# Mixture-of-experts loop: VectorE computes the next pair's weight addresses ahead of its label and meta copies

## What is computed

```python
logits = tokens @ router_weight.T                  # 32 experts, 4 picked for each token
topk_idx, topk_w = _route(tokens, router_weight, router_bias)
gate_vals = silu(einsum('th,eih->tei', tokens, gate_w))
up_vals = einsum('th,eih->tei', tokens, up_w)
expert_out = einsum('tei,ehi->teh', gate_vals * up_vals, down_w)
mixed = (take(expert_out, topk_idx) * topk_w).sum(1)
out = layernorm(x + mixed + shared(x))
```

## Time and profile before

| what | value |
|---|---|
| time, median of 3 runs | 595.2 us (590.54 to 598.46) |
| span of the profiled execution (its own time; no other is listed for it) | 591.0 us |
| TensorE busy, matmuls | 557.3 us, 94% |
| VectorE busy | 372.0 us, 63% |
| ScalarE busy | 278.8 us, 47% |
| GpSimd busy | 289.8 us, 49% |
| mean granted TensorE clock | 0.988 |

### The profile page before, as it was taken

One profiled execution on the slowest core, in us unless ns is written; L12 is line 12 of the kernel. 1 busy time (PEld: TensorE's weight loads), 2 busy tenths in 40 slices (PEclk: granted clock), 3 DMA queues, 4 the chain that ended last, 5 costly groups with the idle time before them and its releaser, 6 DMA issues.

```text
span 591.0 us, 16304 instructions
## 1 busy us (share of the span) xinstructions
PE 557.3 (94%) x4916; PEld 437.1 (74%) x4917; DVE 372.0 (63%) x1250; ACT 278.8 (47%) x561; POOL 289.8 (49%) x301
## 2 busy tenths in 40 slices
PE   5989999999989999999969999999999999999985
PEld 2446578677665766675529999999999999887863
DVE  2032657698885887679544666666666665634774
ACT  2334453765837575253213555555555554530234
POOL 5000000654777765667741666666666665660221
PEclk9999999999999999999987999999999999999998
DMA  7999978987899799799423555555555554528996
GB/s 260 249 237 230 236 220 201 277 271 193 267 248 287 224 322 391 268 395 343 171 93 96 168 165 164 162 172 163 160 167 168 180 171 153 172 91 353 414 413 246
DMA packets 125820, 135.34 MB, mean 229 GB/s; under 512 B 76872, under 2 KB 107087, under 8 KB 125136
## 3 DMA queue, kind: packets, MB, share of 16 engines
q1 hardware_dynamic: 108288, 95.92, 54.3%
q0 software_dynamic: 12672, 34.10, 15.2%
q10 hardware_dynamic: 4816, 4.74, 2.3%
HBM read 74.79 MB, written 60.96 MB: 230 GB/s over the span
## 4 chain that ended last, share of the span: by engine, by line
PE 63%; DMA 15%; SPq 6%; issue 5%; POOL 4%; DVE 3%; ACT 2%; ACTq 0%; POOLq 0%; DVEq 0%
PE bank L933 54%; PE bank L1292 5%; DMA wgu_sb<-pick_rows 4%; DMA o_slots<-wgu_sb 4%; DMA wd_sb<-o_slots 3%; POOL expert_rows L534 3%; PE bank L1350 2%; DMA expert_rows<-stage,pos 2%; SPq L319 1%; SPq L328 1%; SPq L299 1%; PE bank L1348 1%; PE bank L981 1%; DMA q_slots<-wd_sb 1%; SPq L285 1%
## 5 line engine op out<-in xcount | busy, mean ns | idle before, releaser
L568 POOL DMA_INDIRECT pick_rows<-prod,ids x134 | 131.2, 979 | 93.9 <-ACT prod L885 46.2
L534 POOL DMA_INDIRECT expert_rows<-stage,pos x128 | 129.1, 1008 | 57.0 <-issue 34.8
L933 PE MATMUL bank<-prod 128*128 128x128 f32 x1088 | 135.0, 278 | 1.0 <-issue 1.0
L933 PEld LDWEIGHTS bank<-prod 128*128 128x128 f32 x1088 | 128.9, 195 | 1.7 <-issue 1.6
L933 PE MATMUL bank<-wd_sb,wqkv_sb 128*128 128x512 f32 x192 | 91.5, 614 | 6.5 <-DMA wqkv_sb<-in_wqkv 5.9
L1754 DVE COPY prod<-wgu_sb 128x512 f32 x136 | 54.1, 440 | 54.5 <-issue 51.8
L885 ACT ACTIVATE prod<-bank,kept 128x256 f32<-128x256 f32 x136 | 57.0, 470 | 37.7 <-PE bank L933 35.1
L933 PEld LDWEIGHTS bank<-wgu_sb 128*32 128x32 f32 x2048 | 58.6, 136 | 16.8 <-issue 13.6
L933 PE MATMUL bank<-wd_sb,prod 128*128 x272 | 70.1, 380 | 0.8 <-DVE prod L1785 0.8
L933 PE MATMUL bank<-wgu_sb 128*32 128x64 f32 x2048 | 65.8, 296 | 2.2 <-DMA wgu_sb<-k_slots 2.2
L933 PEld LDWEIGHTS bank<-wd_sb,wqkv_sb 128*128 128x128 f32 x192 | 35.1, 194 | 41.6 <-issue 35.8
(11 more groups left out here) (148 smaller groups left out, 774.6 us busy)
## 6 DMA issues: line engine op xcount, KB each, us to landing
prod<-expert_rows SPq DMA_DIRECT2D x136, 132.0 KB
wgu_sb<-pick_rows SPq DMA_DIRECT2D x32, 512.0 KB, 14.7
wgu_sb<-in_wgu SPq DMA_DIRECT2D x2, 2560.0 KB, 13.4
expert_rows<-pad_rows SPq DMA_DIRECT2D x4, 1056.0 KB, 19.0
wd_sb<-in_xT SPq DMA_DIRECT2D x8, 512.0 KB, 4.8
q_slots<-wd_sb SPq DMA_DIRECT2D x16, 256.0 KB
k_slots<-wd_sb SPq DMA_DIRECT2D x16, 256.0 KB
wgu_sb<-q_slots SPq DMA_DIRECT2D x16, 256.0 KB
```

The lines of the kernel that those rows point to most:

```text
L534: pool.indirect_dma_start(xs, bass.IndirectOffsetOnAxis(ap=pos[e % 2][:, i, k:k + 1], axis=0), stage[:, i, k, :], None, bounds_check=XROWS ...
L568: pool.indirect_dma_start(z, bass.IndirectOffsetOnAxis(ap=index[:, j:j + 1], axis=0), rows[:, j, :], None, bounds_check=TOPK * NTOK - 1, o ...
L933: return pe.matmul(dst, lhsT, rhs, start=(k == 0), stop=(k == n - 1))
```

## The change

The register part of `copy_weights` becomes a function of its own, `find_weights`, which loads the packed word and holds the offsets of both tiles in registers. In a pair's body it is called first. The label is no longer the last step of the body, for pair n-1, but follows `find_weights` in the next body, for pair n-2; then come the keep, the meta copy and the weight copies. The last labels stand behind the loop.

```diff
+            def find_weights(quad, slot):
                 word = quad_experts(dve, quad)
+                return [dve.snap(dve.to_reg(expert(word, slot + j) * (KC * 2 * EI)), min_val=0,
+                                 max_val=(NE - 1) * KC * 2 * EI) for j in range(2)]
+
+            def copy_weights(n, par, found):
                 if not (isinstance(n, int) and n < 2):
                     dve.wait_ge(S["cgu_ps"], n - 1)
                 for j in range(2):
-                    last = dve.tensor_copy(ws[par][:, j, :],
-                                           wgu_sb[:, bass.ds(expert(word, slot + j) * (KC * 2 * EI), KC * 2 * EI)])
+                    last = dve.tensor_copy(ws[par][:, j, :], wgu_sb[:, bass.ds(found[j], KC * 2 * EI)])
                 last.then_inc(S["ws_ready"], 1)
...
             def pairs(quad, par, has_prev, has_next):
                 n = quad * 2 + par
+                if has_next:
+                    found = find_weights(quad + par, 0 if par else 2)
+                if not (isinstance(n, int) and n < 2):
+                    dve.wait_ge(S["kept"], n - 1)
+                    label_rows(n - 2, par, quad * 32 - 32)
                 if has_prev:
                     keep_meta(n - 1, 1 - par)
                 if has_next:
                     copy_meta(n + 1, 1 - par, quad + par)
-                    copy_weights(n + 1, 1 - par, quad + par, 0 if par else 2)
+                    copy_weights(n + 1, 1 - par, found)
...
-                if has_prev:
-                    dve.wait_ge(S["kept"], n)
-                    first = isinstance(n, int) and n < 3
-                    label_rows(n - 1, 1 - par, None if first else (quad * 32 if par else quad * 32 - 32))
...
-            copy_weights(0, 0, 0, 0)
+            copy_weights(0, 0, find_weights(0, 0))
             quads_with_ends(dve, quads, pairs)
+            dve.wait_ge(S["kept"], quads * 2 - 1)
+            label_rows(quads * 2 - 2, 0, quads * 32 - 32)
             keep_meta(quads * 2 - 1, 1)
```

More of the change, by code:

```diff
@@ L1747, in copy_meta @@
                 dve.tensor_copy(meta[par][:, :, :], xt[par][:, :, ID:ID + 2]).then_inc(S["cmeta"], 1)
-            def copy_weights(n, par, quad, slot):
+            def find_weights(quad, slot):
                 word = quad_experts(dve, quad)
+                return [dve.snap(dve.to_reg(expert(word, slot + j) * (KC * 2 * EI)), min_val=0,
+                                 max_val=(NE - 1) * KC * 2 * EI) for j in range(2)]
+            def copy_weights(n, par, found):
                 if not (isinstance(n, int) and n < 2):
```

## The result

The changed kernel takes 606.64 us (median of 6 runs, 601.73 to 609.32) against 596.9 us (590.54 to 599.53). The ratio on record is 1.019, with a 95% interval of 1.0145 to 1.023 (the two medians alone give 1.016). The forecast was 612.7 us against 595.2, a ratio of 1.029. So the sign is right, the time lies in the range, and the loss is 10 to 11 us where 17.5 were forecast. The change is slower beyond doubt; whether by more than 2% this interval leaves open.

A forecast was written before the change was run, and what follows sets the result against it. TensorE was taken to set the rate, VectorE as good as level. Terms of 0.26 + 0.29 us less 0.025 slack, 0.53 in two pairs, times 32, gave 17 us: 608.5 us span, 612.7 us with the median's offset; range 594.5 to 634.

The forecast's parts named there:

- The bound: Loop: TensorE sets the rate, 3.09 us a pair; VectorE nearly level, 0.02 to 0.03 us spare in 6.18.
- The two terms: VectorE, second product to first weight copy: +0.26 us in the body without the branch, +0.29 us with it.
- T + 1.35: Body without the branch: the label starts 1.35 us after T, the start of the second product before it.
- the 0.4 + 0.15 of the forecast: Body without the branch: 0.4 us from label to meta copy, then 0.15 us from meta to the weight copies.
- What follows: VectorE from the first weight copy on: copies and two products stay the same, nothing added.
- The reason given: VectorE: the edit hides 0.42 us of finding behind the product but uncovers more: label, keep, meta, second tile's arithmetic.
- rival 1: Between product and copies: the finding disappears behind the product, not slower, 592 to 595 us; chance 0.27.
- best case: Body without the branch: tile arithmetic fuses, extra wait free; copy at 1.45 us, 0.2 below before; no gain in time.
- Rival 2: VectorE's finding: arithmetic and bounds check for each held offset, 0.28 us each, 35 us more, 648; chance 0.07.
- Rival 3: Labels wait at the port shared with GpSimd until its scatter ends; 3.3 us a pair, 13 us more, 608; chance 0.09.
- Late row loads: SyncE's loads come later with the meta copy, still covered by 0.4 us or more before TensorE's transposes; no cost.

The follow-up runs named there:

- e4b_fixed_places: Kernel before without the word's load and register arithmetic, copying two fixed experts' weights; ratio 0.996 to the kernel before (0.999 on the first, slow chip).
- e6b_second_load: Kernel before with the word's load, address and bounds check done twice; ratio 1.061 to the kernel before (0.967 on the first, slow chip).
- e8_keep_one_port: Changed kernel with the keep done by a sum over an axis of one instead of a copy; ratio 1.003 to the kernel before.
- e7b_word_only: Changed kernel holding only the word early, each tile's place worked out at its copy; ratio 0.997 to the kernel before.
- e2_label_back: Changed kernel with the label back at the body's end, right behind the second product; ratio 1.030 to the kernel before.
- e1b_find_late: Changed kernel with the finding put back behind the meta copy, both places held; ratio 1.035 to the kernel before (0.951 on the first, slow chip).

## Why the prediction was right, and where not

**The bound, right.** It took the steady 3.09 us for TensorE's rate and VectorE for level with it. e4b_fixed_places shows the first (a lighter VectorE gains 0.4%), e6b_second_load the second (1.10 us more in the steps, 1.0 in the period). This was the step that decided that the loss would show at all.

**The two terms, right in sum, wrong in part.** Product to first copy was forecast at 1.93 and 2.33 us and measured at 2.00 and 2.30; the sum of the terms was 0.55 and came out at 4.30 - 3.74 = 0.56. But 0.23 us of the 2.00 is the keep that GpSimd's indirect DMA held. Without it the step is 1.77 (e8_keep_one_port). The finding and the waits ahead of the label were overestimated: the label was forecast at T + 1.35 and starts 432.56 - 431.34 = 1.22 us behind the product. From the label to the copy it is 433.34 - 432.56 = 0.78, less the 0.23 of the hold 0.55, which is the 0.4 + 0.15 of the forecast. The hold, which the sum left out, made up for the overestimate: that 0.55 and 0.56 agree is in part luck.

**What follows, mis-sized.** The prediction put this term at nothing: "what follows (copies, two products) stays the same". It did not stay the same. From first copy to second product it went from 1.18 and 1.26 us to 1.16 and 1.13 in the mean. Between the two copies only the address operation of 0.05 is left of the 0.19 of arithmetic. In the body with the branch, before, an operation of 0.04 for a count stood ahead of the second product (L1784), and it is gone. 0.15 us in two pairs, times 32, is 5 us, most of the gap between the 17 us forecast for the loop and the 11.7 measured. The rest lies in the first and last pairs: 208.1 us are 1.1 more than 33.5 times the steady 6.18, and 219.8 are 0.9 less than 33.5 times 6.59.

**The reason given, half right.** "What it uncovers is label, keep, meta and the second tile's arithmetic, which is more" puts four things in one sum. The experiments part them. With the load ahead and the arithmetic left at the copies, product to first copy is shorter than before by 0.19 and 0.11 us (e7b_word_only), with no gain in time, as rival 1 said. So what label, keep and meta lose is less than what the early load hides. The loss needs the held places: they add 0.30 and 0.32 us to the way to the first copy (1.77 and 2.29 in e8_keep_one_port, 1.47 and 1.97 in e7b_word_only). The prediction had the second tile's arithmetic in it as 0.19 and the address operation as a possible 0.1, and did not see that without these two its own steps come to some 1.65 us, level with the 1.67 before. Its best case of 1.45 lies next to the 1.47 measured in e7b_word_only, but by luck: there the label starts 0.86 us behind the product and the copy 0.62 behind the label, where the best case had 0.98 and 0.47.

**The rivals.** Rival 2, a bounds check for each held value: no row shows one. Rival 3, the port: the label never waits (0.17 us in both bodies), but the keep behind it does. The mechanism is there, with a smaller price than a whole scatter: 0.23 us in one body of two. For the time it matters more than its chance of 0.09 says: without it the changed kernel is at 1.003. Late row loads: the transposes didn't wait for them in the steady loop, as forecast. ScalarE's waits for scatters (39.1 us between 350 and 500 us) were not foreseen; they lie beside VectorE's cycle, and without them e2_label_back is no faster.

**Beating both.** e7b_word_only has a shorter VectorE cycle than the kernel before and the same time within its interval. Even with all finding left out (e4b_fixed_places) the ratio is 0.996: less work on VectorE has nothing more to gain while TensorE takes 3.09 us a pair.

## What to carry to other kernels

- An engine with 63% busy can be level with the bottleneck: look at its sequencer's rows and at whether its first waiting instruction waits at all. The gap of 0.03 us told more than the share.
- When register work is moved to the front, move the load and its wait, not the arithmetic that already lies beside a copy; here a value held in a register also cost an address operation of 0.05 us at each copy, where place and address were one operation before.
- A reordering also moves the other engines' instructions against each other. Before blaming or crediting the order, list the instructions that got longer and compare their ends with those of the neighbour.

## What the runs showed of the hardware

**Held copies.** In the changed kernel the keep of 4 elements a partition took 0.40 us and ended with GpSimd's indirect DMA; the same values by a sum over an axis of one took 0.16 at the same point of the DMA. In e1b_find_late the order of starts can be seen to decide who is held. GpSimd and VectorE in it, at two places (at the second the row has both weight copies, of 0.43 us each; the idle time before the copies, which the profile puts down to TensorE, is filled with the load and the arithmetic):

```profile
406.47 0.97 POOL L568 DMA_INDIRECT pick_rows<-prod,ids  x1 [0.99 <-DVE ids L1765]
406.98 0.71 DVE L1758 COPY prod<-wgu_sb 128x512 f32 x1 [1.14 <-PE bank L933]
...
392.73 1.04 POOL L568 DMA_INDIRECT pick_rows<-prod,ids  x1 [0.99 <-DVE ids L1765]
393.23 0.77 DVE L1758 COPY prod<-wgu_sb 128x512 f32 x2 [1.12 <-PE bank L933]
```

A weight copy that began 0.51 us into an indirect DMA took 0.71 instead of 0.43 and ended 0.25 behind it. One that began 0.49 us into one took its 0.43, and then it was the indirect DMA that was late: 1.04 us long instead of 0.97, with its end 0.12 behind the copy's. All 22 copies of this kernel that begin 0.46 to 0.56 us into an indirect DMA, between 350 and 500 us, fall on either side of 0.51 in this way. So in these runs the DMA holds a copy only from the middle of its record. In e2_label_back a weight copy that runs from 0.32 to 0.75 us of a record leaves both at their usual length. The Trainium skill, page "SBUF — State Buffer", section "SBUF: two separate sides", says that a VectorE operation in a two-port mode and GpSimd take the shared ports exclusively, whoever starts first, for the whole instruction. The common ends, the sum that is never held and the switch at 0.5 us, with either side held in its turn, agree with such a lock. That copies get through in the first half of a record doesn't agree with "the whole instruction", if the record is the instruction.

**A chip on which a slower engine helps.** On one chip the kernel before took 731.77 us, and a second word load, 0.6 us more work a pair, made it 3.3% faster. The same two kernels on another chip are 6.1% apart the other way. Some 79 us of that chip's extra time lie ahead of the loop (first transposes at 387.9 us in e4_fixed_places, 309.1 in the kernel before on the other chip), where the mean granted TensorE clock is 0.89 up to 309 us, against 0.99. So a verdict on a 2% change may not carry over from one chip to another; what did was the length of each step on VectorE (e1: 1.98 and 2.35 on one, 1.99 and 2.35 on the other).
